# The last two batches of a fused decoder layer: the order of the program's end, and two VectorE passes for gain and offset

## The reference

```
x = LN(x + attention(x))                 # 16 heads of 32, low-rank terms on q, k, v, o
x = LN(x + x * scan(ctx*ctx, decay))     # running sum r = d*r + c*c along the tokens
h = gelu(silu(bitlinear(x, w1, b1)))     # 512 -> 2048
h = (h - mean(h)) * rsqrt(var(h)+eps) * ln_g + ln_b
x = LN(x + bitlinear(h, w2, b2))         # 2048 -> 512
```

## Time and profile before

| | us |
|---|---|
| median of 3 runs | 1041.54 (1039.56 to 1042.92) |
| the profiled execution | 1039.61 |
| its span, first to last instruction | 1037.8 |
| TensorE busy in the span | 941.8 (91%) |
| VectorE busy | 859.1 (83%) |
| ScalarE busy | 826.3 (80%) |
| GpSimd busy | 548.5 (53%) |

### The profile page before, as it was taken

One profiled execution on the slowest core, in us unless ns is written; L12 is line 12 of the kernel. 1 busy time (PEld: TensorE's weight loads), 2 busy tenths in 40 slices (PEclk: granted clock), 3 DMA queues, 4 the chain that ended last, 5 costly groups with the idle time before them and its releaser, 6 DMA issues.

```text
span 1037.8 us, 23337 instructions
## 1 busy us (share of the span) xinstructions
PE 941.8 (91%) x9244; PEld 647.8 (62%) x9260; DVE 859.1 (83%) x1490; ACT 826.3 (80%) x957; POOL 548.5 (53%) x767
## 2 busy tenths in 40 slices
PE   5998987999999999999999999999999999977515
PEld 3766756676777667676767767676767777654102
DVE  4578868889797989889897979898897979897766
ACT  3646686888989798888888897988889897977684
POOL 2332338274654639373755647383746546472643
PEclk9999998999999999999999999999999999999768
DMA  9432200313132222323141212323131412122213
GB/s 361 158 113 113 73 3 21 75 49 88 22 85 52 55 62 56 81 53 85 27 110 22 75 46 61 71 53 85 52 85 22 97 40 75 22 63 54 53 34 89
DMA packets 106351, 73.67 MB, mean 71 GB/s; under 512 B 91385, under 2 KB 91385, under 8 KB 104450
## 3 DMA queue, kind: packets, MB, share of 16 engines
q1 hardware_dynamic: 105522, 70.34, 25.3%
q10 hardware_dynamic: 720, 1.84, 0.5%
HBM read 41.73 MB, written 8.40 MB: 48 GB/s over the span
## 4 chain that ended last, share of the span: by engine, by line
DVE 33%; PE 25%; ACT 17%; issue 13%; POOL 7%; DMA 3%; SPq 1%; DVEq 0%; ACTq 0%; POOLq 0%
PE bank L1484 8%; PE bank L1345 7%; DVE neg_max L965 6%; POOL h L549 5%; DVE stats L1022 3%; ACT h L727 3%; DVE h L1096 3%; ACT junk L737 3%; ACT h L742 3%; DVE fz L1101 2%; DVE qk_parts L988 2%; PE bank L1485 2%; ACT L727 2%; DVE rows L1038 2%; DVE qx L1063 2%
## 5 line engine op out<-in xcount | busy, mean ns | idle before, releaser
L965 DVE TENSOR_REDUCE neg_max<-wave 128x8 f32<-128x2048 f32 x64 | 146.2, 2284 | 29.4 <-PE wave L1370 29.4
L549 POOL TENSOR_TENSOR h<-h,g_tile 128x2048 f32<-128x2048 f32 x30 | 139.2, 4640 | 39.1 <-ACT h L742 39.1
L659 ACT ACTIVATE probs<-wave 128x1024 f32<-128x1024 f32 x128 | 124.2, 1023 | 28.2 <-PE wave L1394 27.9
L1484 PE MATMUL bank<-w,xqT 128*128 128x512 fp8e4 x496 | 130.0, 385 | 17.5 <-DMA xqT<-xq 13.6
L439 POOL TENSOR_SCALAR attn_hi<-attn 128x256 fp32r<-128x256 f32 x64 | 28.3, 442 | 174.3 <-DVE attn L1004 159.4
L697 ACT ACTIVATE rows<-rows,rstd 128x512 f32<-128x512 f32 x96 | 74.4, 807 | 41.9 <-POOL rstd L455 23.7
L1096 DVE TENSOR_TENSOR h<-h,b_tile 128x2048 f32<-128x2048 f32 x32 | 84.1, 2629 | 18.6 <-POOL h L549 18.0
L721 ACT ACTIVATE h<-bank,qx 128x512 f32<-128x512 f32 x124 | 82.3, 689 | 20.0 <-PE bank L1485 16.7
L1491 PE MATMUL bank<-w,hqT 128*128 128x512 fp8e4 x416 | 94.3, 380 | 0.3 <-DMA hqT<-h 0.3
L1484 PEld LDWEIGHTS bank<-w,xqT 128*128 128x128 bf16 x496 | 46.7, 99 | 74.9 <-DMA xqT<-xq 9.9
L1345 PE MATMUL bank<-xT_hi,wq_hi 128*128 128x256 f32 x256 | 78.8, 308 | 0.1
(11 more groups left out here) (184 smaller groups left out, 2736.9 us busy)
## 6 DMA issues: line engine op xcount, KB each, us to landing
ctx_sb<-ctxT SPq DMA_DIRECT2D x16, 512.0 KB, 3.7
rows<-x SPq DMA_DIRECT2D x16, 512.0 KB, 4.0
out<-rows SPq DMA_DIRECT2D x32, 256.0 KB, 2.1
xT_in<-xT SPq DMA_DIRECT2D x15, 512.0 KB, 4.0
h<-w1T SPq DMA_DIRECT2D x4, 1024.0 KB, 14.0
h<-w2T SPq DMA_DIRECT2D x4, 1024.0 KB, 5.0
h<-Wq SPq DMA_DIRECT2D x1, 1024.0 KB, 5.9
h<-Wk SPq DMA_DIRECT2D x1, 1024.0 KB, 9.4
```

Source lines behind the costliest of these rows:

```text
L549: po.tensor_tensor(h_of(b, q)[:, :], h_of(b, q)[:, :], g_tile[:, :], ALU.mult).then_inc(done, 1)
L659: ac.activation(probs[:, kt, :, :], wave[:, :, kt * T:(kt + 1) * T], ACT.Exp, scale=SM_SCALE).then_inc(S["probs_ready"], 1)
L965: dv.tensor_reduce(neg_max[:, :, :], wave[:, :, :].rearrange("p j (t k) -> p j t k", t=NT), axis=AX_X, op=ALU.max, negate=True).then_inc(S ...
L1484: pe.matmul(p[:, :], xqT[:, q, kc, :], w1[:, kc, n * FW:(n + 1) * FW], start=(kc == 0), stop=False)
```

## The change

The last `body(j)` stops early on ScalarE, VectorE, TensorE and, for some steps, GpSimd; what it leaves is taken up by a `drain()` in another order. Gain and offset of batches 14 and 15 are computed otherwise: `center` computes (h + (-mean)) * ln_g, `scale_add` computes that times 1/deviation plus ln_b, each as two VectorE instructions of 1024 columns; `h_norm`, `gain`, `z_add` and GpSimd's `g_mul` are gone for them. Batch 15's input rows go to the buffer xT_in, and its one-column results to a new `fs_last`. On ScalarE all eight silu pieces of batch 15 come before the first gelu of batch 14. The attention output product of batch 15 is cut in pieces between the last attention steps, and other PSUM banks are given out.

The diff, cut (the new waits and bank numbers in part):

```diff
 def load_rows(b):                                   # SyncE
+    if b == LAST:
+        wait(sp, "x_lo", LAST, 1); wait(sp, "res1", PRIOR, 1)
...
 def drain():                                        # SyncE
+    transpose_z(THIRD, 0)
+    transpose_x(LAST)
     transpose_z(THIRD, 1)
-    transpose_x(LAST)
     store_out(THIRD, 0)
     store_out(THIRD, 1)
     transpose_z(PRIOR, 0)
...
 def drain():                                        # GpSimd
-    neg_mean(PRIOR, 0)
-    neg_mean(PRIOR, 1)
     inverse_std1(LAST)
     inverse_std2(LAST)
     x_rms(LAST)
-    h_rstd(PRIOR, 0)
-    h_rstd(PRIOR, 1)
+    z_rms(THIRD, 1)
+    drain_neg_mean(PRIOR, 0)
     inverse_std3(THIRD, 0)
+    drain_rstd(PRIOR, 0)
+    drain_neg_mean(PRIOR, 1)
+    drain_rstd(PRIOR, 1)
+    wait(po, "z_added", PRIOR, 4)
     inverse_std3(THIRD, 1)
-    g_mul(PRIOR, 1)
     res2(PRIOR)
     res2(LAST)
     z_rms(PRIOR, 0)
...
 def drain():                                        # ScalarE
-    zq_store(THIRD, 1)
+    zq_store(THIRD, 0)
+    silu(PRIOR, 0, (0, 1))
     normalise(1, LAST, 0)
     normalise(1, LAST, 1)
...
+def center(b, q):                                   # VectorE
+    dv.wait_ge(d_stat, stat_count(b, q) + 1)
...
+    for i, part in enumerate(centered(q)):
+        cols = slice(i * INNER // 2, (i + 1) * INNER // 2)
+        dv.scalar_tensor_tensor(part, h_of(b, q)[:, cols], fs_of(b)[:, q, H_NMEAN:H_NMEAN + 1],
+                                g_tile[:, cols], ALU.add, ALU.mult).then_inc(d_center, 1)
+
+def scale_add(b, q):
+    dv.wait_ge(d_stat, stat_count(b, q) + 3)
+    for i, part in enumerate(centered(q)):
...
+        last = dv.scalar_tensor_tensor(h_of(b, q)[:, cols], part, fs_of(b)[:, q, H_RSTD:H_RSTD + 1],
+                                       b_tile[:, cols], ALU.mult, ALU.add)
+    last.then_inc(S["z_added"], 1)
...
 def drain():                                        # VectorE
+    attn_norm(LAST, 3)
+    quantise_z(THIRD, 0)
+    scan(LAST)
     layernorm1_sum(LAST, 0)
     layernorm1_sum(LAST, 1)
+    z_add(THIRD, 1)
     layernorm2_sum(LAST, 0)
     layernorm2_sum(LAST, 1)
+    z_max(THIRD, 1)
+    quantise_x(LAST)
+    quantise_z(THIRD, 1)
     layernorm3_sum(THIRD, 0)
+    center(PRIOR, 0)
+    scale_add(PRIOR, 0)
+    z_max(PRIOR, 0)
+    center(PRIOR, 1)
+    scale_add(PRIOR, 1)
+    z_max(PRIOR, 1)
     layernorm3_sum(THIRD, 1)
-    quantise_x(LAST)
...
     quantise_z(PRIOR, 0)
+    center(LAST, 0)
+    scale_add(LAST, 0)
+    center(LAST, 1)
+    z_max(LAST, 0)
+    scale_add(LAST, 1)
+    quantise_z(LAST, 0)
     quantise_z(PRIOR, 1)
...
 def drain():                                        # TensorE
+    drain_o(0, (0, 1))
+    shiftT(LAST, 3)
+    drain_o(1, (0, 1))
+    shifted(LAST, 3)
+    drain_o(0, (2,))
+    drain_o(1, (2,))
+    weighted(LAST, 3)
+    drain_o(0, (3,))
+    drain_o(1, (3,))
```

More of the change, by code:

```diff
@@ L314, in load_rows @@
             def load_rows(b):
-                wait(sp, "out_stored", b - NROWS, 32)
+                if b == LAST:
+                    wait(sp, "x_lo", LAST, 1)
+                    wait(sp, "res1", PRIOR, 1)
+                else:
+                    wait(sp, "out_stored", b - NROWS, 32)
                 sp.dma_start(rows_of(b)[:, :, :],
@@ L593, in body @@
                     x_lo(j + 1)
+                else:
+                    res1(LAST)
                 if alive(j, 0):
@@ L713, in zq_store, with silu @@
                               bias=neg_round[:, :]).then_inc(S["zq_stored"], 1)
-            def silu(b, q):
-                for n in range(NF):
+            def silu(b, q, tiles=range(NF)):
+                for n in tiles:
                     u = NF * q + n
@@ L905, in drain @@
             def drain():
-                zq_store(THIRD, 1)
+                zq_store(THIRD, 0)
+                silu(PRIOR, 0, (0, 1))
                 normalise(1, LAST, 0)
                 normalise(1, LAST, 1)
-                h_var(PRIOR, 0)
-                h_var(PRIOR, 1)
+                silu(PRIOR, 0, (2, 3))
+                silu(PRIOR, 1)
                 normalise(2, LAST, 0)
                 normalise(2, LAST, 1)
-                h_norm(PRIOR, 0)
+                z_square(THIRD, 1)
@@ L914, in drain @@
                 xq_store(LAST)
-                h_norm(PRIOR, 1)
-                normalise(3, THIRD, 0)
-                normalise(3, THIRD, 1)
-                silu(LAST, 0)
-                z_square(PRIOR, 0)
-                silu(LAST, 1)
-                z_square(PRIOR, 1)
-                gelu(LAST, 0)
-                gelu(LAST, 1)
-                h_var(LAST, 0)
-                h_var(LAST, 1)
-                h_norm(LAST, 0)
-                h_norm(LAST, 1)
-                zq_store(PRIOR, 0)
+                zq_store(THIRD, 1)
@@ L1086, in z_add @@
             def z_add(b, q):
[L1088 to L1093 removed]
+                wait(dv, "g_mul", b, q + 1)
                 if b == 0:
@@ L1130, in quantise_z @@
                 else:
-                    for i, done in ((0, d_round), (1, S["z_quant"])):
+                    for i, done in ((0, d_round), (1, d_quant)):
                         half = h_of(b, q)[:, i * INNER // 2:(i + 1) * INNER // 2]
@@ L1298, in drain @@
-                quantise_x(LAST)
-                gain(PRIOR, 0)
-                z_add(PRIOR, 0)
-                z_max(PRIOR, 0)
-                z_add(PRIOR, 1)
-                z_max(PRIOR, 1)
-                quantise_z(PRIOR, 0)
-                quantise_z(PRIOR, 1)
-                gain(LAST, 0)
-                z_add(LAST, 0)
-                z_max(LAST, 0)
-                z_add(LAST, 1)
-                quantise_z(LAST, 0)
+                center(PRIOR, 0)
+                scale_add(PRIOR, 0)
```

186 lines of the change are left out of this document (129 added, 57 removed).

## The result

The changed kernel took 1052.87 us in the median of four runs (1052.21 to 1054.38), the kernel before 1041.71 beside it (1039.56 to 1042.92): a ratio of 1.0103, with a 95% interval of 1.0084 to 1.0121, so **slower by 1.0%**. The forecast was 1054 us. The profiled execution took 1052.67 with a span of 1050.7, against 1039.61 and 1037.8.

A forecast was written before the change was run, and what follows sets the result against it. No engine bounds the whole; the end is a dependency chain mostly through VectorE. Batch 15 13.1 us earlier, batch 14 5.1 later, then waits and serial y: span 1050.7 (12.9 more), execution 1052.5, plus 1.93: 1054 us, range 1046 to 1058.

The forecast's parts named there:

- Part 1: Last attention group to batch 15's silu: f starts at 965.0, last silu ends at 975.9 against 989.0, 13.1 us earlier.
- the held rstd1: Layer norm 1 of batch 15: GpSimd's one-column power slowed beside VectorE's z_add(13,1), charged 2.2 us more.
- Part 2: Batch 14's gelu behind all silus on ScalarE: VectorE's first pass for it starts at 979.7 instead of 974.6, 5.1 later.
- Part 3: VectorE's list from 979.7, fused passes 1.22 apart, with waits for GpSimd: norm3(13,1) done at 1023.5.
- The large wait: VectorE stands still 7.3 us before quantise_z(14,0), to 1005.0, for z_rms(14,0) queued behind res2 on GpSimd.
- Part 4: SyncE and TensorE: transposes wait behind the store of (13,1), y starts at 1027.3, four in a row to 1043.7, span 1050.7.
- the tail behind the last y: From the last y's end to the end of the span: 7.06 us, as in the kernel before.
- the 1.93 added for the median: The kernel before's median lay 1.93 us above its profiled execution; added to 1052.5, giving 1054.4.
- A: Rival on GpSimd at the end: its instructions are not held by VectorE's passes; inside the range, chance 0.15.
- B: Rival on VectorE's fused passes of 1024 columns: 0.71 us each, the lower bound, instead of 1.22; chance 0.06.
- C: Rival at z_rms(14,0) behind res2: GpSimd's results always in time, span 1039.7 or 1037.8, not slower; chance 0.08.
- D: Rival at the end: late-landing transposes 1.3 us apart, more than one tile at low clock (1.9 each), 1060; chance 0.11.

The follow-up runs named there:

- run 3: Changed kernel with z_add(13,1) and z_max(13,1) on VectorE behind quantise_x(15), and z_square(13,1) behind xq_store on ScalarE: 1054.12 us, ratio 1.0105.
- Run 4: Changed kernel with batch 14's two gelus and deviations ahead of batch 15's silus on ScalarE: 1041.92 us, ratio 0.9997.
- run 5: Changed kernel with inverse_std3(13,0) and the four res2 additions on GpSimd moved behind z_rms(13,1), into VectorE's idle time at 967: 1047.62 us, ratio 1.0065.
- Run 1: Changed kernel with SyncE's store of (13,1) issued behind the eight last transposes instead of ahead: 1050.23 us, ratio 1.0077.
- run 6: Kernel before, in its old order, with only the fused passes center and scale_add, and two waits on GpSimd: 1033.85 us, ratio 0.9919.
- run 7: Changed kernel with the 16 fused passes replaced by one-input tensor_scalar passes, leaving out ln_g and ln_b of batches 14 and 15: 1047.82 us, ratio 1.0054.
- Runs 8: Changed kernel reordered on ScalarE, GpSimd and VectorE, gelus of batch 14 before silu, res2 split, store of (13,1) last: 1030.24 us, ratio 0.9891.
- run 10: The reordered version (Runs 8) with gelu(14,0) ahead of zq_store(13,1) and both res2 gated by waits on GpSimd: 1028.25 us, ratio 0.9860.
- run 2: Changed kernel with GpSimd's four res2 additions moved right behind z_rms(13,1), at about 960: 1051.32 us, ratio 1.0085.

## Why the prediction was right, step by step

It was right in its path; what it had in each step against what the trace shows:

- **Part 1** (batch 15 earlier): attn_norm(15,3) 935.1, measured 935.90; f(15) 965.0 and 965.53; last silu 975.9 and 977.87. Silus wait for f's groups, and TensorE was at its lower clock of 1.2 GHz behind 7.57 us of idleness (granted 0.50 from 965.5 to 969.5, 1.00 from 971.6 on): they came 2.14 and 1.76 apart at first and 1.08 later, where before only one step, of 1.43, was long. One printed sum lacks a term: 949.2 + 3.3 + 4.0 + 4.3 is 960.8, not 961.6; the 0.8 is norm1 up to the first sum. The trace has 12.36 from norm1's start to the end of quantise_x, as the 12.4 had it. The 2.2 us for the held rstd1 were 1.95 (2.14 less 0.19), and run 3 shows z_add as the cause.
- **Part 2** (batch 14 behind it): first fused pass 979.7, measured 981.49, all of it from the silus. Run 4 shows this order to be worth 11 us. My text called it 5.1 later than before and set no price on the 15.5 us of idleness ahead of it: the step was right, its weight only implied.
- **Part 3**: a fused pass costs 1.28, 1.20 from start to start (I took 1.22). The waits for deviations were smaller, 1.07 and 0.44 instead of 2.0 and 1.1: GpSimd got its turns between the halves of center, not only behind both. The large wait was 7.23 instead of 7.3 and ended with z_rms on GpSimd; run 5 took 4.9 of it away. norm3(13,1) ended at 1023.14, forecast 1023.5.
- **Part 4**: transposes at 1023.60 (1024.0), y(14,0) at 1028.27 (1027.3: landing took 4.67 from the first issue, not 3.25), four y's in a row to 1044.41 (1043.7). Run 1 shows the store's part, 2.4. The landing could have been read: in the kernel before, the transposes of (14,0) were issued at 1006.14 and its y began at 1010.93, 4.79 later. SyncE's row there:

```profile
1006.14 2.61 SPq L336 DMA_TRANSPOSE hqT<-h  x2
```

The span of 1050.7 is met to the tenth by luck: the first pass (1.8) and the landing (1.4) were set too early, the waits (1.6, and 0.3 before scale_add(15,1) that did not come) and the tail behind the last y (7.06, measured 6.3) too long. What was left of the miss in the time, 1054 against 1052.87, is the 1.93 added for the median: here the median lay 0.2 above the profiled execution.

The fusion, which the prediction entered by its lengths alone, is a gain (run 6), as it said. The two additions of ln_b that took 6.49 us beside GpSimd's product are gone in that trace, and so are four passes of ScalarE; how the 7.4 us divide between them is not shown. Against that the rewritten order lost 1.70% by runs 1, 4 and 5, some 18 us.

Of the rivals, **A** (GpSimd not held) is out: its power took 1.40 beside the first fused pass. **B** (0.71 a pass) is out with 1.28; its price of 6.3 was well set, since in run 7 y(14,0) came 6.1 earlier (and the first y took 0.7 longer, so that the span fell by 5.4). **C** (results always in time) is out: VectorE waited 8.74 us behind the first fused pass (1.07, 7.23 and 0.44). Runs 8 and 10 come near it, with 2.2 and 3.2 us from the first fused pass to the last rounding. **D** is out in its larger part (more tiles at the low clock): only the first y took 5.77. Its late landing did come, with 1.4 us.

On the hold, the Trainium skill ("SBUF — State Buffer", section Who interferes with whom) says more than the prediction drew from it: a tensor_scalar in its two-port mode contends with GpSimd too, a tensor_reduce on trn2 never does, and whoever issues first keeps the ports for the whole instruction. The rows agree: 1.16 beside tensor_scalar (run 7), 2.49 for two additions at full speed beside z_max (run 10). My expectation of run 7 was wrong where it left the first of these out.

## What to carry to other kernels

A fused or faster operation and a new order of queues should be tried apart: here one gained 0.8% and the other lost 1.7 to 1.8%. When an engine's idle time is long, ask which queue has the producer behind something that isn't ready; and put a store that waits for a late result behind the transfers that feed the path. Work moved to an idle engine isn't free if the two hold each other, as VectorE and GpSimd do here: give it the other's idle time or an operation that doesn't hold, and gate it there by a wait.

## What the hardware showed that was not expected

- GpSimd's 128x512 additions (1.24 each) hold VectorE's smallest instructions, casts and tensor_tensor of 2 to 6 columns: 0.92 to 1.20 instead of 0.17 (run 2). One addition, one hold: each small instruction loses its turn again.
- A one-input instruction of GpSimd on 128x2 is held for a whole pass of VectorE, 2.14 instead of 0.19. Not every one is: in the changed kernel those at 981.53 and 1013.28 took 0.19 inside fused passes, and runs 1 to 4 repeat it. Nothing here shows what sets them apart.
- How long the first y takes after a pause (3.62 us at full clock) isn't set by the pause alone. After 42.45, 42.47 and 42.80 us of idle TensorE it took 4.96, 6.49 and 6.21 (runs 5, 7, 2), after 18.3 to 19.2 us 4.90 to 4.96 (runs 6, 8, 10), after 34.07 us 6.53 (run 4), after 47.68 and 49.15 us 5.77 and 5.56 (changed kernel, run 3). No run here isolates what sets it, and it moves a single profiled span by up to 1.6 us, so gains of that size are better read at the start of y(14,0).
